# Context attention of a perceiver layer: DMA transposes for the tokens, a ring of four groups, and three pieces of work moved between engines

## What is computed

```python
xn = layernorm(ctx, ln_x_g, ln_x_b)           # ctx (32, 1601, 256)
ln = layernorm(latents, ln_l_g, ln_l_b)       # latents (32, 64, 256)
q = ln @ W_q
kv = concatenate([xn @ W_kv, ln @ W_kv], axis=1)
k, v = kv[..., :256], kv[..., 256:]           # 4 heads of 64
sim = einsum('bhid,bhjd->bhij', rmsnorm(q, q_gamma) * SCALE, rmsnorm(k, k_gamma))
sim = where(full_mask, sim, -max)
out = einsum('bhij,bhjd->bhid', softmax(sim), v)
x = x + out @ W_out + b_out
x = x + self_attention(layernorm(x)); x = x + ffn(layernorm(x))
```

## Time and profile before

| | us |
|---|---|
| median of 3 runs | 1211.06 (1209.39 to 1211.7) |
| profiled execution: span of its instructions | 1207.6 |
| context stage in it | about 198 to 467 |
| PE busy in the whole span | 954.6 (79%) |
| DVE busy | 778.5 (64%) |
| ACT busy | 536.4 (44%) |
| POOL busy | 373.9 (31%) |

### The profile page before, as it was taken

One profiled execution on the slowest core, in us unless ns is written; L12 is line 12 of the kernel. 1 busy time (PEld: TensorE's weight loads), 2 busy tenths in 40 slices (PEclk: granted clock), 3 DMA queues, 4 the chain that ended last, 5 costly groups with the idle time before them and its releaser, 6 DMA issues.

```text
span 1207.6 us, 29932 instructions
## 1 busy us (share of the span) xinstructions
PE 954.6 (79%) x10867; PEld 648.7 (54%) x10867; DVE 778.5 (64%) x1523; ACT 536.4 (44%) x898; POOL 373.9 (31%) x287
## 2 busy tenths in 40 slices
PE   4366544788888886867788787878599999999997
PEld 3233333566666665646767686767344544544444
DVE  6867764888888885765989888888541342421412
ACT  0145543555544544534555545555443353343332
POOL 4356665333334435751121212121240030210300
PEclk9988866888878877888999989989799999999999
DMA  4133322222222221320101101010000000000000
GB/s 141 32 99 100 102 82 75 72 78 78 70 76 81 69 69 36 71 59 2 50 26 48 46 25 48 24 48 26 26 1 1 18 0 0 17 0 0 18 1 19
DMA packets 61653, 55.31 MB, mean 46 GB/s; under 512 B 22424, under 2 KB 57121, under 8 KB 61601
## 3 DMA queue, kind: packets, MB, share of 16 engines
q1 hardware_dynamic: 61601, 54.60, 15.0%
HBM read 44.09 MB, written 10.49 MB: 45 GB/s over the span
## 4 chain that ended last, share of the span: by engine, by line
PE 47%; DVE 20%; issue 14%; POOL 9%; ACT 4%; DVEq 2%; DMA 1%; SPq 1%; ACTq 0%; POOLq 0%
PE ps L1247 25%; PE ps L1639 16%; POOL tmp L426 2%; POOL rstd L458 2%; PE ps L1518 2%; DVE big L1018 2%; DVE sm L1155 2%; POOL big L434 1%; DVE tmp L1150 1%; PE ps L1547 1%; POOL tmp L494 1%; DVE stats L952 1%; DVE tmp L1157 1%; PE ps L1367 1%; DVE tmp L1160 1%
## 5 line engine op out<-in xcount | busy, mean ns | idle before, releaser
L1247 PE MATMUL ps<-tmp,wat 128*128 (+1 forms) x1536 | 111.2, 244 | 49.4 <-DVE tmp L1160 26.0
L1247 PEld LDWEIGHTS ps<-tmp,wat 128*128 128x128 bf16 x1536 | 107.4, 111 | 52.8 <-issue 50.6
L1247 PE MATMUL ps<-tmp 128*128 128x128 bf16 (+2 forms) x1056 | 127.2, 279 | 1.6 <-DVE tmp L984 1.4
L1639 PE MATMUL ps<-wat,big 128*128 128x512 bf16 x512 | 111.2, 379 | 5.7 <-ACT tmp L785 5.7
L1639 PE MATMUL ps<-tmp,big 128*128 128x512 bf16 x512 | 113.8, 379 | 1.2 <-POOL tmp L531 1.2
L1247 PE MATMUL ps<-tmp,big 128*128 128x512 bf16 (+2 forms) x448 | 105.2, 398 | 2.0 <-ACT tmp L707 1.3
L1247 PEld LDWEIGHTS ps<-tmp 128*128 128x128 bf16 x1056 | 90.9, 117 | 14.1 <-issue 7.3
L531 POOL TENSOR_TENSOR tmp<-tmp 128x512 bf16<-128x512 f32 x32 | 37.0, 1158 | 184.4 <-DVE tmp L1214 184.4
L515 POOL TENSOR_TENSOR big<-d_rn,maskb 128x256 bf16<-128x256 f32 x20 | 13.4, 672 | 244.8 <-ACT maskb L725 244.8
L1639 PEld LDWEIGHTS ps<-wat,big 128*128 128x128 bf16 x512 | 49.8, 98 | 67.1 <-issue 5.8
L1220 DVE TENSOR_TENSOR tmp<-tmp 128x512 bf16<-128x512 f32 x32 | 22.1, 692 | 94.7 <-ACT tmp L785 94.7
(11 more groups left out here) (215 smaller groups left out, 2265.4 us busy)
## 6 DMA issues: line engine op xcount, KB each, us to landing
big<-in_wff SPq DMA_DIRECT2D x16, 704.0 KB, 4.0
tmp<-in_ctx SPq DMA_DIRECT2D x80, 128.0 KB, 2.1
tmp<-q_scr SPq DMA_DIRECT2D x72, 128.0 KB, 2.0
big<-in_wat SPq DMA_DIRECT2D x16, 256.0 KB, 2.7
q_scr<-big SPq DMA_DIRECT2D x16, 256.0 KB, 2.6
xres<-in_x SPq DMA_DIRECT2D x1, 2048.0 KB, 8.6
v_scr<-big SPq DMA_DIRECT2D x16, 128.0 KB, 1.7
p_scr<-big SPq DMA_DIRECT2D x16, 128.0 KB, 1.8
```

The source lines that it names most:

```text
L1247: last = pe.matmul(to, left(l), right(r), start=start and k == 0, stop=k == len(pairs) * len(passes) - 1)
L1639: last = pe.matmul(ps[4 + m % 2][:, :], w[:, l, c, m * P:(m + 1) * P], hb[layer][:, r, c], start=k == 0, stop=k == len(passes) * HC - 1)
```

## The change

Only the context stage changes. What it does:

- TensorE no longer transposes tokens. SP issues two DMA transposes for a group (`turn_tokens`), SBUF to SBUF, each of [128 x 1024] bfloat16 into eight blocks of 128 by 128: one for the high parts and one for the low parts. The copies out of PSUM (`b_tokens`) are gone, and the transposed tokens are double-buffered.
- The split tokens live in a ring of four groups, addressed with a register, in place of two fixed buffers.
- Normalisation is on ScalarE: four activations with a scale and a bias for each row (`b_norm`), with the bias from one small VectorE instruction (`b_shift`). `b_moments` has five operations in place of seven.
- Both halves of the tokens' low part are on GpSimd, and so is the second half of the probabilities' low part; `b_scale` is two instructions of 8 columns in place of one of 16.
- Sum and count: the products and the column of ones go into a pair of adjacent PSUM banks, and VectorE adds both in one operation of 514 columns.
- `b_stats` and `b_deviations` run three groups ahead, ScalarE's squares stand between the two halves of the exponential, SP reads its lists ahead of its waits, and queries are loaded a group ahead.

The core of the diff:

```diff
+            def turn_tokens(slot, h, l, w1):
+                sp.wait_ge((q.b_hi, q.b_lo)[l], w1)
+                sp.sem_inc(q.gate, 1)
+                sp.dma_start_transpose(xct[h][:, l].rearrange("p i c n -> p (i c) n"),
+                                       ring[:, ds(slot, 1), l].rearrange("p s i n -> p (s i n)")).then_inc((b_th, b_tl)[l][h], 16)
...
             with sp.Fori(0, count, 2 * G) as w:
+                later = sp.snap(((w >> 2) + 2) & 2)
                 for h in range(2):
-                    sp.wait_ge(q.b_s, w + h * G)
-                    load_q(w + h * G)
-                    load_x(w + (h + 2) * G, h, w + (h + 1) * G)
+                    at = w + h * G
+                    rows_at = rows_of(at + 4 * G)
+                    load_q(at + G, at + G)
+                    sp.wait_ge(q.b_k, at + G)
+                    sp.sem_inc(q.gate, 1)
+                    for l in range(2):
+                        turn_tokens(later + h, h, l, at + 3 * G)
+                    load_x(rows_at, h)
...
@@ gpsimd
-                po.tensor_tensor(sm2[:, :], sm1[:, :], neghalf[:, 0:AH], ALU.pow).then_inc(q.b_rr, G)
+                for k in range(2):
+                    half = slice(k * AH // 2, (k + 1) * AH // 2)
+                    po.tensor_tensor(sm2[:, half], sm1[:, half], neghalf[:, 0:AH // 2], ALU.pow).then_inc(q.b_rr, G // 2)
...
                 for h in range(2):
-                    b_deviations(w + (h + 3) * G)
-                    b_low(w + (h + 3) * G, h)
-                    b_scale(w + (h + 2) * G)
+                    at = w + h * G
+                    b_low(at + 3 * G, later + h, h)
+                    b_deviations(at + 4 * G, 1 - h)
+                    b_probs_low(at + G)
+                    b_scale(at + 2 * G)
...
@@ scalar
+            def b_norm(w1, slot, h):
+                act.wait_ge(q.b_sh, w1)
+                for i in range(G):
+                    act.activation(xt[h][:, i], xt[h][:, i], ACT.Identity, bias=cshift[h][:, i:i + 1],
+                                   scale=crs[h][:, i:i + 1]).then_inc(q.b_n, 1)
+                for k in range(2):
+                    half = slice(k * G // 2, (k + 1) * G // 2)
+                    act.wait_ge(q.b_n, w1 - (1 - k) * G // 2)
+                    act.activation(ring[:, ds(slot, 1), 0, half].rearrange("p s i n -> p (s i n)"), flat(xt[h][:, half]),
+                                   ACT.Copy).then_inc(q.b_hi, G // 2)
...
-                    b_high(at + 2 * G, 1 - h, 1, True)
-                    b_tokens(at + 2 * G)
-                    b_exp(at, columns)
-                    act.wait_ge(q.b_ss, at + G)
+                    b_norm(at + 3 * G, later + h, h)
+                    b_exp(at, columns, 0)
+                    b_keys_squared(at + 2 * G)
+                    b_exp(at, columns, 1)
                     act.wait_ge(q.b_s, at + G)
                     b_keys(at + 2 * G)
-                    b_high(at + 3 * G, h, 0, True)
...
@@ vector
-                sums, ones = acc[:, ds(batch, 1), :], accs[:, ds(batch, 1), :]
-                v.tensor_tensor(flat(sums), flat(sums), ps[0 if i % 2 == 0 else 7][:, :], ALU.add)
-                v.tensor_tensor(flat(ones), flat(ones), ps[1 if i % 2 == 0 else 4][:, 0:HP], ALU.add).then_inc(q.b_acc, 1)
+                sums = flat(acc_sums[:, ds(batch, 1), :])
+                v.tensor_tensor(sums, sums, pairs[i % 2][:, 0:SUMS], ALU.add).then_inc(q.b_acc, 1)
...
@@ tensor
-            def b_transpose(w1, h):
-                pe.wait_ge(q.b_lo, w1)
-                pe.wait_ge(q.b_lo2, w1)
...
+            def b_keys(w1, h):
+                pe.wait_ge(b_th[h], 2 * w1 + (1 - h) * 8)
...
+                pe.wait_ge(b_tl[h], 2 * w1 + (1 - h) * 8)
...
                     pe.wait_ge(q.b_acc, at - 1 if h == 1 else at)
-                    b_transpose(at + 2 * G, 1 - h)
-                    b_keys(at + 2 * G)
-                    b_products(at, h)
+                    b_keys(at + 2 * G, 1 - h)
+                    b_products(at, base + h)
```

More of the change, by code:

```diff
@@ L32 @@
 GT = G * P
-LW = NT + 4 * G
+LW = NT + 6 * G
+SUMS = 2 * D + HP
+RING = 4
 BB = 5
@@ L106, in build @@
         tmp = sb("tmp", [P, 40 * 256], F32)
-        ps = [ctx.enter_context(nc.psum_tensor(f"ps{i}", [P, 512], F32)) for i in range(8)]
+        pairs = [ctx.enter_context(nc.psum_tensor(f"pp{i}", [P, 1024], F32)) for i in range(2)]
+        ps = [pairs[i // 2][:, i % 2 * 512:i % 2 * 512 + 512] for i in range(4)]
+        ps += [ctx.enter_context(nc.psum_tensor(f"ps{i}", [P, 512], F32)) for i in range(4, 8)]
         def carve(area, at, words, dt=F32):
@@ L344, in _ @@
                 a_step(k, k % 2)
+            sp.wait_ge(q.a_lo, RT)
+            sp.wait_ge(q.a_t, RT)
+            for h in range(2):
+                rows_at = rows_of((h + 2) * G)
+                for l in range(2):
+                    turn_tokens(h, h, l, (h + 1) * G)
+                load_x(rows_at, h)
             sp.wait_ge(q.a_qst, 16 * RT)
@@ L551, in _ @@
             act.wait_ge(q.small_in, 16 * 8)
-            act.activation(bo[:, 0, :], bof[:, :], ACT.Copy).then_inc(q.bo_hi, 1)
+            act.activation(bo[:, 0, :], bof, ACT.Copy).then_inc(q.bo_hi, 1)
             def a_step(k, p):
@@ L628, in _, with b_keys_squared @@
             count = act.value_load(wn[0:1, 0:1], min_val=1, max_val=NT)
-            def b_tokens(w1):
-                act.wait_ge(q.b_t, w1)
-                act.activation(xct[:, 0].rearrange("p c n -> p (c n)"), ps[0][:, :].bitcast(BF16),
-                               ACT.Copy).then_inc(q.b_eh, G)
+            def b_keys_squared(w1):
+                if not isinstance(w1, int):
+                    act.wait_ge(q.b_ss, w1 - G)
+                for c in range(HP):
+                    act.wait_ge(q.b_k, w1 - (HP - 1 - c) * G // HP)
+                    act.activation(ksq[:, c], ps[4 + c][:, :], ACT.Square,
+                                   bias=bk[:, c:c + 1]).then_inc(q.b_ksq, G // HP)
@@ L635, in b_keys @@
             def b_keys(w1):
                 for c in range(HP):
-                    act.wait_ge(q.b_k, w1 - (HP - 1 - c) * G // HP)
-                    act.activation(ksq[:, c], ps[2 + c][:, :], ACT.Square,
-                                   bias=bk[:, c:c + 1]).then_inc(q.b_ksq, G // HP)
-                for c in range(HP):
-                    act.activation(kct[:, 0, c], ps[2 + c][:, :], ACT.Identity,
-                                   bias=bk[:, c:c + 1]).then_inc(q.b_khi, G // HP)
-            def b_exp(w, columns):
-                act.wait_ge(q.b_sn, w + G)
-                act.wait_ge(q.b_pv, w)
-                for k in range(2):
-                    half = slice(k * G // 2, (k + 1) * G // 2)
-                    for i in range(half.start, half.stop):
-                        act.activation(pr[:, i], pr[:, i], ACT.Exp, bias=maskb[:, ds(columns[i], 1)]).then_inc(q.b_p, 1)
-                    act.wait_ge(q.b_p, w + half.stop)
-                    act.activation(flat(prh[:, half]), flat(pr[:, half]), ACT.Copy).then_inc(q.b_ph, G // 2)
@@ L655, in _, with b_exp @@
-            b_tokens(G)
+                    act.activation(kct[:, 0, c], ps[4 + c][:, :], ACT.Identity,
+                                   bias=bk[:, c:c + 1]).then_inc(q.b_khi, G // HP)
+            def b_exp(w, columns, k):
+                act.wait_ge(q.b_sn, w + (k + 1) * G // 2)
+                if k == 0:
+                    act.wait_ge(q.b_pv, w)
+                half = slice(k * G // 2, (k + 1) * G // 2)
+                for i in range(half.start, half.stop):
+                    act.activation(pr[:, i], pr[:, i], ACT.Exp, bias=maskb[:, ds(columns[i], 1)]).then_inc(q.b_p, 1)
+                act.wait_ge(q.b_p, w + half.stop)
+                act.activation(flat(prh[:, half]), flat(pr[:, half]), ACT.Copy).then_inc(q.b_ph, G // 2)
@@ L1400, in b_scores, with b_products @@
                             at = (i % 2) * D + h * P
-                            last = product(ps[5 + k][:, at:at + P],
+                            last = product(ps[6 + k][:, at:at + P],
                                            [(lambda l: kct[:, l, h, i * P:(i + 1) * P], lambda r: qc[:, i, 2 * r + h, :])])
                     last.then_inc(q.b_s, G // 2)
-            def b_products(w, h):
-                parts, probs = (xch[h], xcl[h]), (prh, prl)
+            def b_products(w, slot):
+                probs = (prh, prl)
+                parts = ring[:, ds(slot, 1)].rearrange("p s l i n -> p (s l) i n")
                 for i in range(G):
```

231 lines of the change are left out of this document (113 added, 118 removed).

## The result

The changed kernel takes 1195.14 us (median of 4 runs, 1194.68 to 1195.9) against 1210.35 for the kernel before beside it (4 runs, 1209.39 to 1211.7): a ratio of 0.987, 95% interval 0.986 to 0.989. The forecast was 1166, a gain of 45 us; the gain is 15. The direction and the range held; two thirds of the forecast gain are missing.

The account below looks back on a forecast made before the run. VectorE's queue, with TensorE close behind, was taken to bound the kernel before at 14.16 us a group. SP's 11.3 plus 0.3 gave 11.6, 46 us less over 18 groups, 1 more ahead of the loop: 1166 us, range 1138 to 1208.

Parts of the forecast that it names:

- The bound of the kernel before and the relief of VectorE: Context loop: VectorE's queue sets the 14.16 us period, TensorE close behind; VectorE's load falls from 12.2 to 7.0 us a group.
- The other engines: Context loop, per group: TensorE 9 to 10.8 us, ScalarE 8.4 busy and 10.3 with open list reads, GpSimd 8.1.
- SyncE's term: SP's queue in the context loop: 9.1 us of issues and reads plus 2.2 of transposes, 11.3 us a group, the largest term.
- interlock: Context loop: loss added because queues this close together don't interlock without loss, 0.3 us a group.
- X: SP's time for one DMA transpose, twice a group: taken as 1.1 us, between bounds of 0.5 and 4.0.
- third rival: SP's queue is the bound and each transposed block costs an issue: X 2.66 to 4.0 us, 1216 to 1265 us; chance 0.10.
- second rival: Context loop: X of 1.6 to 2.4 us or late transfers, 12.3 to 14 us a group, 1178 to 1208 us; chance 0.20.
- The head: Ahead of the loop: tokens wait for GpSimd and a transfer, transposes and copies go; 1 us more, bounds -2 and +4.
- The end: After the context loop: nothing changes, 0 us.
- The transfers: DMA transposes' data: 1.7 us for two of 256 KB over 16 engines, with most of a group to land in.
- fourth rival: Transposes' transfers not spread over the DMA engines: 13.5 us each, 27 us a group, 1442 us in all; chance 0.07.
- The ring: Context loop: an order of waits through TensorE, VectorE, GpSimd and ScalarE, 10.1 us a group, under SP's 11.3.

Follow-up runs that it names:

- e2: The changed kernel with the first group's queries issued ahead of the head's four DMA transposes and token loads: 1194.81 us.
- e6: The changed kernel with SP taking four batch numbers from one packed read and the first queries issued ahead of the first transposes: 1170.02 us.
- e5: The changed kernel with one DMA transpose of sixteen blocks a group in place of two of eight: 1189.20 us.
- e10: The changed kernel with packed batches, token rows from two reads, first queries early and one DMA transpose of sixteen blocks a group: 1157.29 us.
- e1: The changed kernel with SP taking a group's four batch numbers from one packed list read in place of four reads: 1175.48 us.

## Why the prediction was right or wrong

**The bound of the kernel before and the relief of VectorE: right.** VectorE's load fell from 12.2 us a group to 155.8 / 18 = 8.7, not to 7.0. Most of the difference is a slip in the working. The busy times of the groups in the earlier trace rows count again what lies under an instruction of another group, the total of 219.4 does not: all groups of VectorE in that stretch sum to 247.1 us, 27.7 above the total, and after to 165.1 against 155.8, 9.3 above. Taking the groups' times off the total took (27.7 - 9.3) / 18 = 1.0 us a group too much. The bias instruction, put at the 0.145 us of a small one, is another 0.4:

```profile
L1014 DVE SCALAR_TENSOR_TENSOR mv<-mv,rstd 128x4 f32<-128x4 f32 x18 | 10.2, 568 | 0.0
```

At 8.7 of 12.77 it decided nothing.

**The other engines: right.** TensorE 191.9 / 18 = 10.7 us (9 to 10.8 forecast), ScalarE 8.5 (8.4), GpSimd 7.8 (8.1; its power of four columns took 1.01 and not 1.36). The clock's mean was 0.86, before 0.85. What addresses in registers cost TensorE no run tells apart; its busy time stayed in the forecast. The gap ahead of ScalarE's normalisation, put at 2 us and down to open list reads, was (18.4 + 6.6) / 18 = 1.4 us, and in 11 of 17 times it ended with VectorE's bias, not with ScalarE's own queue:

```profile
ACT tmp L657 <- DVE mv L1014: 18.4, 11, 2.1
...
ACT tmp L657 <- issue: 6.6, 6, 1.7
```

**SyncE's term: the right engine, mis-sized, and that is the step that failed.** The forecast had 9.1 us of issues and reads and 2.2 of transposes, 11.3 in all, and named SP as the largest of its terms. The trace has 12.99 in one group, 12.96 in the mean of SP's own queue:

| per group | forecast | measured from start to start |
|---|---|---|
| eight issues | 4.0 | 2.33 + 2.54 = 4.9 |
| eight reads | 5.1 | 5.2 |
| two transposes | 2 x 1.1 = 2.2 | 2.9 |
| interlock | 0.3 | 0 |
| sum | 11.6 | 13.0 |

Half of the error is in the issues: 1.88 us for four was read from the start of the first to the end of the last, and divided to 0.5; from start to start it is 0.53, and the gates, waits and loop registers ahead of the first were in no row that I counted. The trace of before had them all in one number: SP waited 72.1 us in 16 groups, 4.5 in each, so 14.16 - 4.5 = 9.7 us of such a group were SP's work, not 9.1; without the transposes' 2.9 the changed kernel has 10.1. The other half is X: 1.47 us from start to start where 1.1 was forecast, twice a group. I took a value nearer to an ordinary issue because the program has one instruction. The one instruction is charged by its blocks, as the third rival had it, but at 0.15 us each and not at 0.33. The bounds for X, 0.5 and 4.0, held it, and 1.26 us lay in the forecast's own range; the period of 12.77 lies in the second rival's (12.3 to 14).

In the account the loop lost 28.0 us where 46 were forecast, 18 too few. A period 1.17 us longer than forecast makes 18 x 1.17 = 21; the difference of 3 lies most likely in where the head ends and the loop begins, since the first scores came late and the next three groups behind them closer together (at 219.21, 230.63, 241.26 and 253.24, 11.3 us each).

**The head: wrong, +10.35 us where +1 with bounds of -2 and +4 was given.** I priced what the keys' path gained and lost there, and that was right: the first keys came at 200.25, before at 202.47. What I left out is what SP's queue does to the queries. Each of their issues now stands behind four transposes and two loads. I hadn't followed that queue through the head. By e2 order alone doesn't win it back; with SP made lighter (e6) up to 5 us may be its share.

**The end: wrong, +3.0 where 0 was forecast.** Its place is seen in the trace (ScalarE, L725, starts 4.3 us after the last sum, on SP's last signal). No run took it away, so its share in the time stays argued.

**The transfers and the fourth rival.** A transpose of 256 KB lands after 3.3 us at the median, not 13.5; TensorE's waits for it are short in the loop (1.8 us in all for L1399). The Trainium skill's page "VectorE: DVE Perf Modes", section "The three transpose paths", has 1309 ns for one block; an estimate by it, if blocks add up, is 10.5 us for eight, and this trace has 3.3 with the latency in it. The Trainium skill's page "DMA: Bandwidth & Descriptors", section "Latency and other measured facts", gives 261 GB/s; eight further blocks took 1.0 us (e5), 262 KB in 1.0 us or some 260 GB/s, read from landings in tenths of a us, and so far page and trace agree.

**The ring.** It was put at 10.1 us. In e10 the period is 11.11 with SP still first in the chain, so the ring's size isn't shown, only that it is no more than that. With TensorE's transposes the period is 12.5 and the chain of waits runs through TensorE, ScalarE and GpSimd, TensorE being 90% busy; there the engines seem to bind each other, but no run takes the three apart.

## What to carry to other kernels

A queue that only issues transfers is an engine like the others: sum its instructions from start to start, register steps, list reads and waits included, before anything is moved onto it. The quickest check of that sum is its period less its waits in the trace of before. Here a move that relieved the two busiest engines was worth -10 us or +21 us (up to 5 of them the queries'), by nothing but five list reads fewer on SP and the first queries' place. When SP never waits in the loop, its integers are the cheapest time in the kernel: four numbers in one word, two rows in one word, the first queries early and one long transfer in place of two took 38 us off with no work changed on any other engine in the loop.

## What was not expected of the hardware

- A DMA transpose of [128 x 1024] bfloat16 holds SP's queue for 1.26 us, one of [128 x 2048] for 1.8 to 3.1 us, 1.9 at the median. After a short one of these an issue takes up to 0.96 us in place of 0.35 (L331 in e5): a part of the cost moves into the instruction behind.
- It lands after 3.3 us (8 blocks) and 4.3 us (16 blocks), and brings some 1,100 packets: the DMA queue had 61,601 packets before and 105,569 after, with 40 transposes and a few loads more. The engines' busy share over the span rose only from 15.0% to 20.3%:

```profile
q1 hardware_dynamic: 105569, 66.66, 20.3%
```

- A read of one number from a list costs SP 0.27 us as an instruction and 0.63 us with what follows it; an idle one, whose number nobody uses, 0.54.
- GpSimd's power takes 1.01 us for 4 columns and 1.64 for 8; one of 16 took 2.90 before. Two of 8 cost 0.4 us more than one of 16, and that was hidden.
- TensorE's granted clock doesn't order the kernels: over the loop it is 0.86 in the changed kernel and in e1, which is 20 us faster, 0.98 in e5 and 0.95 in e10 (215 to 425 or 430 us), and e5, with the highest, is 32 us slower than e10. With the faster clock TensorE was busy 158.7 of 215 us in e5, 176.7 in the changed kernel; SP set the period in both. The row is e5's:

```profile
215.00:430.00 215.00, 158.71 (x1564) 118.03 (x1564) 148.62 (x338) 144.97 (x275) 129.19 (x103) 0.98 0.49 122
```
